# Second attention: the turned maxima and the query rows summed on TensorE, and read out by ScalarE in 26 of 32 slots

## The reference, cut to what matters

```python
qkv = x @ Wqkv.T + bqkv
qkv = qkv.reshape(b, n, 16, -1).transpose(0, 2, 1, 3)
q, k, v = jnp.split(qkv, 3, axis=-1)          # 16 heads of 8 features
scores = jnp.einsum('bhqd,bhkd->bhqk', q, k) / 8 ** 0.5
attn = jax.nn.softmax(scores, axis=-1)
out = jnp.einsum('bhqk,bhkd->bhqd', attn, v)
```

## Time and profile before

| what | value |
|---|---|
| three runs, median | 553.9, 556.0, 558.52 us; 556.0 us |
| profiled execution, its own time | 559.11 us |
| its span in the trace | 557.4 us |
| TensorE matmul, busy | 520.1 us (93%), 3801 instructions |
| VectorE, busy | 407.5 us (73%) |
| ScalarE, busy | 340.4 us (61%) |
| mean granted TensorE clock | 0.975 of full |
| second attention in the trace | about 259 to 397 us |

### The profile page before, as it was taken

The page is one execution under the profiler, slowest core; times in us unless marked ns, Lnnn a source line. Parts: engine busy times, 40 slices in busy tenths (PEclk is TensorE's granted clock), DMA queues, the critical chain, the costliest instruction groups (busy, mean ns, idle before and its releaser), DMA issues.

```text
span 557.4 us, 11771 instructions
## 1 busy us (share of the span) xinstructions
PE 520.1 (93%) x3801; PEld 394.2 (71%) x3801; DVE 407.5 (73%) x1098; ACT 340.4 (61%) x606; POOL 337.9 (61%) x429
## 2 busy tenths in 40 slices
PE   7888989998999999998878989898899999999997
PEld 7666556877888888885545656555578888888885
DVE  4678797676787886676787886978278686686564
ACT  3777766665565556555567675656855655555553
POOL 5897683698767877684613042230488685776663
PEclk9999999999999999999699997969999999999999
DMA  7486870732634233347423344110433444364241
GB/s 178 138 268 192 256 226 5 132 115 67 127 121 127 78 133 92 114 130 246 151 80 102 128 133 125 52 36 2 83 110 110 94 140 123 97 142 131 86 146 38
DMA packets 48566, 67.60 MB, mean 121 GB/s; under 512 B 6641, under 2 KB 18946, under 8 KB 48514
## 3 DMA queue, kind: packets, MB, share of 16 engines
q1 hardware_dynamic: 45408, 66.47, 41.1%
q10 hardware_dynamic: 3106, 0.48, 0.5%
HBM read 53.56 MB, written 13.37 MB: 120 GB/s over the span
## 4 chain that ended last, share of the span: by engine, by line
PE 67%; ACT 11%; DVE 7%; POOL 6%; issue 5%; DMA 3%; SPq 1%; POOLq 0%; DVEq 0%; ACTq 0%
PE bank L1006 15%; PE bank L1008 15%; PE bank L1007 15%; ACT PT L885 6%; PE bank L1128 4%; PE bank L1183 4%; PE bank L1160 2%; DVE PT L1571 2%; POOL KS L745 2%; DMA head_rows<-PHI 2%; PE bank L1013 1%; DVE MEXP L1588 1%; PE bank L1107 1%; PE bank L1071 1%; DMA KS<-head_rows 1%
## 5 line engine op out<-in xcount | busy, mean ns | idle before, releaser
L745 POOL TENSOR_TENSOR KS<-PT,QS 128x512 fp32r<-128x512 f32 x143 | 184.6, 1292 | 85.1 <-ACT QS L981 79.5
L976 ACT ACTIVATE bank<-bank 128x512 f32<-128x512 f32 x128 | 74.6, 582 | 103.5 <-PE bank L1008 102.9
L1685 DVE TENSOR_TENSOR PT<-CS,bank 128x512 f32<-128x512 f32 x128 | 87.6, 684 | 57.6 <-PE bank L1008 56.3
L1006 PE MATMUL bank<-XH,WH 128*128 128x512 f32 (+1 forms) x288 | 114.9, 399 | 0.0
L1008 PE MATMUL bank<-XH,WL 128*128 128x512 f32 (+1 forms) x288 | 112.3, 390 | 0.0
L1007 PE MATMUL bank<-XL,WH 128*128 128x512 f32 (+1 forms) x288 | 112.2, 390 | 0.0
L1588 DVE TENSOR_REDUCE MEXP<-bank 128x4 f32<-128x1024 f32 x64 | 78.3, 1224 | 25.4 <-PE bank L1128 24.5
L1690 DVE TENSOR_TENSOR PT<-PT,bank 128x512 f32<-128x512 f32 x128 | 88.0, 688 | 8.3 <-ACT bank L976 0.3
L981 ACT ACTIVATE QS<-PT 128x512 fp32r<-128x512 f32 x144 | 89.9, 624 | 6.2 <-DVE PT L1690 5.9
L885 ACT ACTIVATE PT<-bank 128x1024 f32<-128x1024 f32 x64 | 65.6, 1026 | 41.3 <-PE bank L1160 41.0
L1183 PE MATMUL bank<-PT,V 128*32 128x256 f32 (+1 forms) x1024 | 65.6, 376 | 0.8 <-ACT OTS L899 0.4
(11 more groups left out here) (208 smaller groups left out, 803.9 us busy)
## 6 DMA issues: line engine op xcount, KB each, us to landing
CS<-combine_rows SPq DMA_DIRECT2D x128, 256.0 KB, 3.2
head_rows<-HP SPq DMA_DIRECT2D x28, 256.0 KB, 3.1
QS<-head_rows SPq DMA_DIRECT2D x28, 256.0 KB, 3.0
KS<-head_rows SPq DMA_DIRECT2D x28, 256.0 KB, 3.7
head_rows<-PHI SPq DMA_DIRECT2D x14, 256.0 KB, 3.7
stage<-in_L_ffn_gate_w_dram SPq DMA_DIRECT2D x5, 192.0 KB, 3.9
stage<-in_L_ffn_up_w_dram SPq DMA_DIRECT2D x5, 192.0 KB, 3.9
stage<-in_L_ffn_down_w_dram SPq DMA_DIRECT2D x5, 192.0 KB, 4.5
```

Source lines behind the costliest of these rows:

```text
L745: pool.tensor_tensor(GL[:, (u - 1) % 3, :], GG[:, (u - 1) % 3, :], GH[:, (u - 1) % 3, :].bitcast(f32), ALU.subtract).then_inc(F.gl, 1)
L976: act.activation(TH[:, u, :] if u < SHARED else G[u % 3][:, :], G[u % 3][:, :], ACT.Silu).then_inc(F.th, 1)
L1006: pe.matmul(out, wh, vh, start=start, stop=False)
L1685: dve.tensor_tensor(ab, CS[:, e % CBUFS, :], U[u % 3][:, :], ALU.mult).then_inc(F.b, 1)
```

## The change

`MEXP` becomes a rounded float32 tile (`f32r`), and a rounded copy of the identity matrix, `IDR`, is made once by ScalarE in slot 5 of the first attention. TensorE's `maxima(i)` no longer transposes: it multiplies `MEXP` by `IDR`, which gives the same turned maxima. In 26 of the 32 items it first multiplies `IDR` by the query rows into the same part of the bank `MT`, so that the bank holds the sum; ScalarE then copies the sum to `Q2`, between the exponentials of pair 1 and pair 0 of that slot. In the six items 0, 2, 8, 10, 16 and 18, whose slots (3, 5, 11, 13, 19, 21) have the `biased_rows` on ScalarE, VectorE adds as before.

```diff
-        MEXP = sb("MEXP", [P, 2, 2, P])
+        MEXP = sb("MEXP", [P, 2, 2, P], f32r)
...
+        IDR = sb("IDR", [P, P], f32r)
...
+        s_idr = sem("ident_rounded")
...
+        def queries_by_vector(i):
+
+            return (i + 3) % SLOTS - 1 in PROJECTION_SLOT and (i + 3) // SLOTS + 1 < CHUNKS
+
         PROJECTION_SLOT = {2: 0, 4: 1}
...
-                pool.memset(MEXP[:, :, :, :], 0.0)
+                pool.memset(MEXP[:, :, :, :].bitcast(f32), 0.0)
...
+                def queries_with_maxima(i):
+
+                    if not 0 <= i < ITEMS or queries_by_vector(i):
+                        return
+                    act.wait_ge(A.mt, i + 1)
+                    if i >= 2:
+                        act.wait_ge(A.s2[0], 2 * i - 2)
+                    act.activation(Q2[:, i % 2, :], MT[:, 0:SEQ], ACT.Copy).then_inc(A.q2, 1)
+
...
+                    if n == 5:
+                        act.wait_ge(s_id, 2)
+                        act.activation(IDR[:, :], ident[:, :], ACT.Copy).then_inc(s_idr, 1)
                 else:
                     if n == 3:
                         act.activation(scratch[:, :], NEG[:, 0:1], ACT.Exp)
                     probabilities(1, n - 4)
+                    queries_with_maxima(n - 3)
                     if g - 1 in PROJECTION_SLOT and c + 1 < CHUNKS:
                         biased_rows(c + 1, PROJECTION_SLOT[g - 1], PJ)
                     probabilities(0, n - 4)
...
+                    if i == 0:
+                        pe.wait_ge(s_idr, 1)
+                    cc, j, b = item(i)
                     for t in range(2):
-                        m = pe.transpose(MT[:, P * t:P * (t + 1)], MEXP[:, i % 2, t, :], ident[:, :])
+                        o = SEQ * b + P * t
+                        if not queries_by_vector(i):
+                            pe.matmul(MT[:, P * t:P * (t + 1)], IDR[:, :], QS[:, j, o:o + P], start=True, stop=False)
+                        m = pe.matmul(MT[:, P * t:P * (t + 1)], MEXP[:, i % 2, t, :], IDR[:, :],
+                                      start=queries_by_vector(i), stop=True)
                     m.then_inc(A.mt, 1)
...
                 def queries_with_maxima(i):
 
-                    if not 0 <= i < ITEMS:
+                    if not 0 <= i < ITEMS or not queries_by_vector(i):
                         return
                     cc, j, b = item(i)
                     dve.wait_ge(A.mt, i + 1)
```

## The result

The four runs of the changed kernel took 561.35, 574.14, 571.26 and 562.43 us, with a median of 566.85; before stood at 556.43 beside them. The ratio, 1.010 (95% interval 1.0056 to 1.0143), rests on 561.35 and 562.43 alone: the other two, at a granted clock of 0.948 against 0.977 and 0.974, count as slow runs and are left out, so what half clock costs is understated if anything. Run again with five rounds, the same kernel gave 1.0165 (1.0111 to 1.0219). By these two ratios the change makes the kernel 1.0 to 1.7% slower (their intervals reach from 0.6 to 2.2%); I had forecast no change, 557.1, and a range that ended at 561.5.

A forecast was written before the change was run, and what follows sets the result against it. The second attention was taken as bound by a ring of waits without the add. Terms -0.2 (VectorE), 0 (ScalarE), +1.2 (TensorE), +0.1 (rounded identity) sum to +1.1 us: 556.0 becomes 557.1, no change; range 551.5 to 561.5.

The forecast's parts named there:

- The ring: Second attention: reduction, products, exponential and scores pace each 3.57 us turn; the add lies in a gap of VectorE.
- My -0.2 for slot 33: VectorE's term: losing 26 adds gains on the path only in slot 33, some 0.2 us.
- The rival with VectorE's add in the ring: Pair 1's reductions start 0.33 us earlier in all 26 slots, 8.6 us gained, 548.5; chance 0.06.
- ScalarE: right: ScalarE's term: 26 copies of 0.384 us fit its idle time before pair 0's exponential, smallest gap 0.61; cost 0.
- +0.08 a slot: TensorE's four multiplications at 0.09 us each take 0.36, against 0.28 for two transposes, in 26 slots.
- The price by the transposes' row, the full array: Alternative price of one TensorE multiplication, 0.11 us from four transposes, against 0.08 from rounded score products.
- slots 12 and 18 for covered: Not among the eleven slots where TensorE was taken to be last, so no cost was counted there.
- all odd slots for covered: In odd slots TensorE waits about 0.32 us for ScalarE, so the added +0.08 vanishes there.
- the whole term: TensorE's added multiplications in eleven slots, seven at 0.08 and four at 0.16 us: +1.2 us.
- the rival with uncovered loads: TensorE's weight loads stand uncovered at 0.188 us each, odd slots late too: +8.6 us, 564.5; chance 0.07.
- The clock: Rival: added multiplications keep TensorE's half-clock stretches at full clock; 554.8 for one, 547.8 for all; chance 0.24.
- 0.34 per us of half clock: Price of TensorE's half clock in the second attention, read from slot pairs; 9.3 us for all four stretches.

The follow-up runs named there:

- e2: Changed kernel with ScalarE's 26 copies but without the 52 query multiplications, maxima left out of those items; 560.7 us, ratio 1.007 to the kernel before.
- e5: Kernel before, transposes and VectorE's adds kept, plus the 52 query multiplications, overwritten by the transposes; 558.1 us, ratio 1.004.
- e1: Changed kernel without query multiplications and copies: VectorE adds in all 32 slots, maxima still turned by rounded multiplications; 560.3 us, ratio 1.006 to before.
- e8: The changed kernel itself, run again; 564.5 us, ratio 1.0165 to the kernel before.
- e3: Changed kernel with the 52 query multiplications kept but overwritten, VectorE adding in all 32 slots, no ScalarE copies; 563.7 us, ratio 1.0124 to before.
- e9: Kernel before with the maxima turned by plain unrounded float32 multiplications by the identity instead of transposes; 559.4 us, ratio 1.0056.
- e6: Kernel before with two idle transposes of the identity ahead of the maxima's two in the 16 odd slots; 554.5 us, ratio 0.998.
- e11: Changed kernel with two idle transposes of the identity ahead of the multiplications in the 16 odd slots; 560.2 us, ratio 1.0087 to before.

## Why the prediction was wrong

*The ring and VectorE: right.* Plain turns at full clock kept their time (slot 10: 3.58 both; slot 17: 3.64 and 3.65; slot 25: 3.58 both), so neither the add nor its removal is in the ring. My -0.2 for slot 33 did not come: 3.73 before and after. The rival with VectorE's add in the ring falls by e2.

*ScalarE: right.* 26 copies at 0.384 us, as the row of the same form had it, all in gaps: 0.43 us or more of waiting is left behind each.

*TensorE: the step that failed first, a term mis-sized.* I had the slots, and not the price: "I take 0.09: four are 0.36, +0.08 a slot". Measured are 0.11 from start to start, 0.17 for the first step, and 0.50 to the next work, +0.22. The price by the transposes' row, the full array, was the right one of the two that I stood between. And I compared unlike things: the 0.28 of the two transposes is the distance to the next work, which by the same steps is 0.17 + 0.11; 4 x 0.09 leaves the longer first step out. I had also held slots 12 and 18 for covered; they lost 0.14 and 0.16. At full clock in both traces, slots 12, 14, 16, 18, 20, 24, 26, 32 and 34 lost 0.14 + 0.24 + 0.26 + 0.16 + 0.25 + 0.27 + 0.26 + 0.27 + 0.25 = 2.1 us. I had held all odd slots for covered; slot 27 lost 0.13 (4.16 and 4.29; 4.29 also in e5, but 4.18 in e1 and e2, so the query multiplications cost it), and slot 7 took 3.82 in place of 3.58, but 3.67 in the second profile of the same kernel (e8), which stays open. At half clock the price is doubled, as I had said: in slot 6 the four take 276.96 - 276.05 = 0.91 us, the two transposes took 274.74 - 274.26 = 0.48. TensorE in slot 6 before:

```profile
274.26 0.69 PE L1143 MATMUL bank<-ident,MEXP 128*128 128x128 f32 x2
274.74 1.91 PE L1071 MATMUL bank<-WV,XV 128*128 128x128 f32 x8
```

And after:

```profile
276.05 0.47 PE L1168 MATMUL bank<-QS,IDR 128*128 128x128 f32 x1
...
276.96 2.02 PE L1091 MATMUL bank<-WV,XV 128*128 128x128 f32 x8
```

By e3 and e5 the whole term is 3.0 and 2.8 us, not 1.2; well under the 8.6 of the rival with uncovered loads. With it alone the forecast would have been 557.1 - 1.2 + 2.9 = 558.8, in the range.

*The clock: the step that took it out of the range.* I counted the clock as a rival on one side only: "turns 64 transposes into multiplications. If that keeps one stretch ... at full clock". The sum had no term for it at all, that is, I took the exchange as neutral at worst. It was the reverse: e1, which has nothing but this exchange (and the one copy of the identity, which e5 has too), has 10 us more at half clock and the ratio 1.006; e5 and e9, which undo it in two ways, are at 13.3 and 15.6 us. A bound from both sides at this place would have held the result; my own 0.34 per us of half clock (0.29 over many runs) was good, and 27 us at half clock in the profile showed how much could move.

## What to carry to other kernels

In a stage where every engine waits in a ring, moving work off an engine with gaps gained nothing here, and the engine that takes it must be asked slot by slot for its own gaps: here TensorE had them in most odd slots, and hardly in the even slots with work of other stages. Price a short sequence by the distance from its first instruction to the next work, for the old and the new form alike. And where the profile shows TensorE at half clock for part of a stage, an exchange that looks free in its duration can move that part, so compare the granted clock over many runs, not in one profile.

## What the runs showed that I had not expected

Two transposes and two rounded multiplications of the same tile occupy TensorE for the same 0.28 us, and with the first the clock holds better: 17.8 us at half clock with transposes, 27.9 with rounded multiplications (e1), 10.5 with two more transposes in odd slots (e6), 19.0 in place of 33.8 when the changed kernel gets them (e11). The Trainium skill (TensorE: Matmul & The Clock Gate, PE-mode transpose) says that transposes do not count as activity in the way multiplications do; here, with float32 transposes, the measured effect goes the other way. The time that TensorE takes does not explain the difference: four multiplications with rounded turning take 0.50 us (e3, 29.8 us at half clock), two unrounded ones 0.55 (e9, 15.6). What goes with it in every run is the rounding: all kernels that turn the maxima unrounded lie at 8.9 to 22.3 us, all that turn them rounded at 27.9 to 40.4, but for e11 with its added unrounded transposes. Why that is so is open.

Full-array weight loads follow each other at 0.11 us though each lasts 0.19 (281.71 and 281.82 in slot 7), so the four cost less (0.50) than four loads one behind the other would. That a load lies under a running multiplication on the same rows of the array is shown by the 0.23 us of the triple in the earlier trace rows, not by this 0.11. So the sentence of the Trainium skill that I weighed in the prediction (TensorE: Matmul & The Clock Gate, The mechanism), read as a rule for every load, does not hold for this trace; the same section also says that a load into the background weight buffer is pulled ahead of running multiplications, and with that the trace agrees.
